# The last stage's norms: scalings of the sums moved from VectorE to GpSimd

## The chip, the cores and the metric

The kernel runs on one core of one Trainium2 chip. The metric is the device time of one execution in microseconds; the median of several runs is compared. Five engines take part, each with a queue of its own and tied to the others by semaphores: TensorE (PE in the rows, its weight loads PEld), VectorE (DVE), ScalarE (ACT), GpSimd (POOL), and SyncE (SP), which only starts DMAs.

## What is computed

A decoder layer for 16 sequences of 100 tokens of width 512: causal self attention, cross attention to a context of 361 tokens, and a feed-forward part with eight experts of which each token takes two; a layer norm follows each of the three. The change lies in the last part. Cut to it:

```python
combined = sum over the token's two experts of weight * silu(x @ expert_w[e] + expert_b[e])
out = combined @ proj_w + proj_b
y = x + out
rms = sqrt(mean(y * y) + 1e-6)                  # RMS norm
x = x + norm_w * (y / rms)
m, v = mean(x), var(x)
x = (x - m) / sqrt(v + 1e-5)                    # layer norm
```

All of it is float32. The matrix products are split in a high and a low part, three products for each.

## The kernel before

The kernel runs in three phases on the same core: self attention, cross attention, feed forward. The feed-forward phase sorts the 1600 tokens by expert into 32 slots of 128 rows, multiplies each by its expert's weights, and writes the results to DRAM (`y_d`). Then comes the last stage, which is all that the change touches.

The last stage goes over 13 tiles of tokens (`NT`), 12 of 128 rows and one of 64. A tile t takes this way:

- GpSimd gathers the two expert results of each row from `y_d` by indirect DMA (`gather_results`, L1903, two instructions a tile);
- ScalarE weighs the first (`weigh_first`, L1637), VectorE adds the weighed second (`combine`, L1803, a scalar_tensor_tensor);
- TensorE transposes the tile (L1577), ScalarE copies the high part (`combined_hi`, L1643), VectorE makes the low part (`combined_lo`, L1809);
- TensorE multiplies by the projection (12 matmuls at L71 and a bias matmul at L1599);
- VectorE adds the residual (`residual`, L1817), ScalarE squares and sums (`square`, L1649) into `ss`;
- VectorE adds the constant to the sum (`mean_square`, L1822), GpSimd raises it to -0.5 (`rms`, L1909) into `rr`;
- VectorE multiplies by it and by the norm's weights (`rms_norm`, L1828, a scalar_tensor_tensor), adds the input and sums (L1831), and makes the negative mean (L1834);
- ScalarE sums the squared deviations (`deviation`, L1654) into `dev`;
- VectorE makes the variance (`variance`, L1839), GpSimd raises it to -0.5 (`ln`, L1914) into `rstd`;
- VectorE makes the shift (`mean_shift`, L1844), ScalarE applies the layer norm (`layer_norm`, L1660), and SyncE stores the tile.

The mean squares, variances, roots and shifts work on one column, a number per row. The order of the work is written out by hand: each engine has one loop over t, in which the steps of different tiles stand behind one another, and it takes them strictly in this order. VectorE's iteration t is: `combine(t + 1)`, `combined_lo(t)`, `mean_square(t - 2)`, `residual(t - 1)`, `mean_shift(t - 4)`, `variance(t - 3)`, `rms_norm(t - 2)`. ScalarE's is: `weigh_first(t + 1)`, `combined_hi(t)`, `deviation(t - 3)`, `square(t - 1)`, `layer_norm(t - 4)`. GpSimd gathers tiles 0 to 4 first; its iteration t is `gather_results(t + 5)` (two indirect DMAs, as long as there are tiles), `rms(t - 1)`, `ln(t - 2)`. So the last gather, of tile 12, stands in front of the root of tile 6. TensorE transposes one tile ahead.

The semaphore `ms_set` counts the mean squares and is what `rms` waits for; `var_set` does the same for `ln`. `sq_done` and `dev_done` count ScalarE's sums.

Of the kernel before, what the change touches and what calls it, by code (L numbers as in the profile page):

```python
# [22 lines left out]
ALU = mybir.AluOpType  # L23
# [4 lines left out]
B, S, D = 16, 100, 512  # L28
DC = D // P
BIG = 3.0e38  # L30
LN_EPS = 1e-5
RMS_EPS = 1e-6
# [13 lines left out]
NT = 13  # L46
# [10 lines left out]
def wait(eng, sem, value):  # L57

    if not isinstance(value, int) or value > 0:
        eng.wait_ge(sem, value)  # L60
# [1323 lines left out]
def feed_forward_phase(nc, sem, bank, stage, rank_set, x2_out, x2_d, y_d, pick_d, expert_w, Ehl, expert_b, proj_w, proj_b, norm_w,  # L1384
# [8 lines left out]
    with ExitStack() as ctx:  # L1393
# [18 lines left out]
        ss, rr, rstd = [[small[:, 4 + k * NT + t:5 + k * NT + t] for t in range(NT)] for k in range(3)]  # L1412
        usum, neg_mean, dev, shift = [[small[:, 4 + k * NT + t:5 + k * NT + t] for t in range(NT)] for k in range(3, 7)]
# [52 lines left out]
        ms_set, var_set, shift_set = sem("c_ms_set"), sem("c_var_set"), sem("c_shift_set")  # L1466
        u_rdy, sq_done, rr_set, norm_step, dev_done = sem("c_u_rdy"), sem("c_sq_done"), sem("c_rr_set"), sem("c_norm_step"), sem("c_dev_done")
# [6 lines left out]
        def rows(t):  # L1474
            return P if t < NT - 1 else B * S - P * (NT - 1)
# [202 lines left out]
        def _(dve):  # L1678
# [121 lines left out]
            def combine(t):  # L1800
                n = rows(t)
                dve.wait_ge(r_w1, t + 1)
                dve.scalar_tensor_tensor(out=r_s[0:n, 0, t], in0=r_s[0:n, 1, t], scalar=weight_of(t, 1), in1=r_s[0:n, 0, t],  # L1803
                                         op0=ALU.mult, op1=ALU.add).then_inc(c_rdy, 1)

            def combined_lo(t):
                n = rows(t)
                dve.wait_ge(c_hi, t + 1)
                dve.tensor_tensor(cTl[:, t % 2, :, 0:n], t_bank[t % 2][:].rearrange("p (c t) -> p c t", c=DC)[:, :, 0:n],  # L1809
                                  cTh[:, t % 2, :, 0:n].bitcast(F32), ALU.subtract).then_inc(c_lo, 1)  # L1810

            def residual(t):
                n = rows(t)
                dve.wait_ge(p_done, t + 1)
                if t % 3 == 0:
                    dve.wait_ge(x2_in[t // 3], 16)
                dve.tensor_tensor(u_s[0:n, t], p_bank[t % 2][0:n, :], x2_tile(t), ALU.add).then_inc(u_rdy, 1)  # L1817

            def mean_square(t):
                n = rows(t)  # L1820
                dve.wait_ge(sq_done, t + 1)
                dve.tensor_scalar(rr[t][0:n, :], ss[t][0:n, :], D * RMS_EPS, None, ALU.add).then_inc(ms_set, 1)  # L1822

            def rms_norm(t):
                n = rows(t)
                u = u_s[0:n, t]
                dve.wait_ge(rr_set, t + 1)
                dve.scalar_tensor_tensor(out=u, in0=u, scalar=rr[t][0:n, :], in1=nw_s[0:n, :], op0=ALU.mult,  # L1828
                                         op1=ALU.mult).then_inc(norm_step, 1)
                dve.wait_ge(norm_step, 2 * t + 1)  # L1830
                dve.tensor_tensor_reduce(out=u, in0=u, in1=x2_tile(t), scale=1.0, scalar=0.0, op0=ALU.add, op1=ALU.add,  # L1831
                                         accum_out=usum[t][0:n, :]).then_inc(norm_step, 1)
                dve.wait_ge(norm_step, 2 * t + 2)
                dve.tensor_scalar(neg_mean[t][0:n, :], usum[t][0:n, :], -1.0 / D, None, ALU.mult).then_inc(mv_set, 1)  # L1834

            def variance(t):
                n = rows(t)
                dve.wait_ge(dev_done, t + 1)
                dve.tensor_scalar(rstd[t][0:n, :], dev[t][0:n, :], 1.0 / D, LN_EPS, ALU.mult, ALU.add).then_inc(var_set, 1)  # L1839

            def mean_shift(t):
                n = rows(t)
                dve.wait_ge(rstd_set, t + 1)
                dve.tensor_tensor(shift[t][0:n, :], neg_mean[t][0:n, :], rstd[t][0:n, :], ALU.mult).then_inc(shift_set, 1)  # L1844
# [7 lines left out]
            for t in range(NT + 4):  # L1852
                if t < 2:
                    combined_lo(t)
                if t + 1 < NT:
                    combine(t + 1)
                if 2 <= t < NT:
                    combined_lo(t)
                if 2 <= t <= NT + 1:
                    mean_square(t - 2)  # L1860
                if 1 <= t <= NT:
                    residual(t - 1)
                if t >= 4:
                    mean_shift(t - 4)
                if 3 <= t <= NT + 2:
                    variance(t - 3)
                if 2 <= t <= NT + 1:
                    rms_norm(t - 2)

        @block.gpsimd  # L1870
        def _(pool):
            def split_lo(n):
                pool.wait_ge(w_hi, n + 1 - 2 * PRE)
                pool.tensor_tensor(pieces[n][3], pieces[n][1], pieces[n][2].bitcast(F32), ALU.subtract).then_inc(w_lo[0], 1)

            def gather_slots(j):
                wait(pool, gt_done, j - 2 * NG + 1)
                pool.indirect_dma_start(out=xg[:, j % (2 * NG)], out_offset=None, in_=x2_f,
                                        in_offset=bass.IndirectOffsetOnAxis(ap=tok_s[:, j:j + 1], axis=0)).then_inc(xg_in[j % (2 * NG)], 16)

            pool.memset(ones_s, 1.0).then_inc(set_up, 1)
            pool.memset(half_s, -0.5).then_inc(set_up, 1)
            for k in range(2):
                pool.memset(run[k][:], 0.0).then_inc(set_up, 1)
                pool.memset(tend[k][:], 0.0).then_inc(set_up, 1)
            pool.wait_ge(x2_out, 16 * B)
            pool.wait_ge(tok_set, 1)
            for j in range(NJ):
                gather_slots(j)
                if j == 2 * NG - 1:  # L1890
                    split_lo(2 * PRE)
                    split_lo(2 * PRE + 2)
                if j == 2 * NG:
                    split_lo(2 * PRE + 4)
                if j in (2 * NG + 2, 2 * NG + 3):
                    split_lo(2 * (LATE + j - 2 * NG - 2))
                if j in (2 * E, 2 * E + 1):
                    split_lo(j)

            def gather_results(t):  # L1900
                n = rows(t)
                for k in range(2):
                    pool.indirect_dma_start(out=r_s[0:n, k, t], out_offset=None, in_=y_d,  # L1903
                                            in_offset=bass.IndirectOffsetOnAxis(ap=pick_s[0:n, t, k:k + 1], axis=0)).then_inc(r_in[t], 16)

            def rms(t):
                n = rows(t)
                pool.wait_ge(ms_set, t + 1)
                pool.tensor_tensor(rr[t][0:n, :], rr[t][0:n, :], half_s[0:n, :], ALU.pow).then_inc(rr_set, 1)  # L1909

            def ln(t):
                n = rows(t)
                pool.wait_ge(var_set, t + 1)
                pool.tensor_tensor(rstd[t][0:n, :], rstd[t][0:n, :], half_s[0:n, :], ALU.pow).then_inc(rstd_set, 1)  # L1914

            pool.wait_ge(h_done, NJ)
            pool.wait_ge(set_up, 2)
            pool.wait_ge(pick_in, 32)
            for slot in y_out:
                pool.wait_ge(slot, 16 * NJ // 2)  # L1920
            for t in range(5):
                gather_results(t)
            for t in range(NT + 2):
                if t + 5 < NT:
                    gather_results(t + 5)
                if 1 <= t <= NT:
                    rms(t - 1)
                if 2 <= t:
                    ln(t - 2)
# [105 lines left out]
```

## Time and profile before

| | us |
|---|---|
| median of 3 runs | 1572.05 (1570.88 to 1576.07) |
| the profiled execution | 1567.09 |
| its span in the trace | 1565.3 |
| TensorE busy | 1478.7 (94%) |
| VectorE busy | 949.5 (61%) |
| ScalarE busy | 662.7 (42%) |
| GpSimd busy | 648.6 (41%) |

The busy times are sums over the whole span, over stages with different limits. The last stage begins with the first gather at 1492.64 us and takes up what is left of the span. Times in the rows below count from the span's start.

### The profile page before, as it was taken

The numbers are of one execution on the slowest core, as the hardware profiler recorded it, in microseconds if no ns is written. First come the engines' busy times: TensorE is split into PE (matmuls) and PEld (weight loads), VectorE is DVE, ScalarE is ACT, GpSimd is POOL, SyncE is SP. The second block draws the span as 40 slices with busy tenths as digits, with TensorE's granted clock in tenths as the row PEclk, the third lists the DMA queues.
The fourth block names the chain that finished last, engine by engine and source line by source line (L and its number), as shares of the span: only waits on it lengthen the run. The fifth ranks groups of instructions, "written<-read, shape, count | busy, mean of one in ns | idle before, by whom it ended". The sixth has DMA issues, their size and how long they took to land. (4 is left out here: it accounts for less than half of the span.)

```text
span 1565.3 us, 28124 instructions
## 1 busy us (share of the span) xinstructions
PE 1478.7 (94%) x8673; PEld 1214.4 (78%) x8673; DVE 949.5 (61%) x3585; ACT 662.7 (42%) x1789; POOL 648.6 (41%) x1000
## 2 busy tenths in 40 slices
PE   8999999999999889999999999999999999479996
PEld 7777877877876678888888888888888887367874
DVE  3766566666666676556655666557655665654457
ACT  4443334334343354444434444434444445343346
POOL 1334334324434454434443444344444443374174
PEclk9999999999999999999999999999999999789998
DMA  6321221122142431212112111211121213365373
GB/s 212 110 72 63 90 78 63 73 85 72 52 141 92 151 115 38 72 51 62 52 53 62 56 55 43 61 56 55 43 62 56 65 40 117 135 212 185 124 233 117
DMA packets 60748, 139.76 MB, mean 89 GB/s; under 512 B 10165, under 2 KB 20761, under 8 KB 59666
## 3 DMA queue, kind: packets, MB, share of 16 engines
q1 hardware_dynamic: 56086, 123.85, 24.0%
q0 software_dynamic: 4576, 14.95, 3.3%
q8 instruction: 32, 0.52, 0.1%
q14 instruction: 54, 0.44, 0.1%
HBM read 94.31 MB, written 44.46 MB: 89 GB/s over the span
## 5 line engine op out<-in xcount | busy, mean ns | idle before, releaser
L1277 POOL TENSOR_TENSOR b_pcarry<-b_half 128x1 f32<-128x1 f32 x173 | 47.9, 277 | 387.5 <-DVE b_rinv L1147 349.8
L1035 ACT ACTIVATE b_probs<-b_probs,b_nmax 100x361 f32<-100x361 f32 x256 | 152.1, 594 | 81.5 <-DVE b_nmax L1141 81.1
L71 PE MATMUL bank<-b_kTh,b_q 128*100 128x362 f32 x512 | 171.8, 337 | 9.1 <-DVE b_kTl L1123 5.8
L1141 DVE CUSTOM_DVE_ANT_0 b_probs<-bank,b_mask 100x361 f32<-100x361 f32 x256 | 135.5, 529 | 52.8 <-issue 45.0
L1302 POOL TENSOR_SCALAR b_probs<-b_probs,b_rinv 100x361 f32<-100x361 f32 x256 | 163.3, 651 | 0.0
L1134 DVE TENSOR_TENSOR b_pTl<-bank,b_pTh 121x400 fp32r<-121x400 f32 x192 | 109.7, 572 | 50.9 <-ACT b_pTh L1030 50.9
L1030 ACT ACTIVATE b_pTh<-bank 121x400 fp32r<-121x400 f32 x192 | 96.5, 503 | 88.4 <-PE bank L867 84.2
L1076 ACT ACTIVATE b_oTh<-bank,b_bv 128x400 fp32r<-128x400 f32 x64 | 38.1, 595 | 223.1 <-PE bank L71 223.1
L867 PE MATMUL bank<-ident,b_probs 100*121 100x100 f32 x768 | 109.8, 265 | 4.3 <-POOL b_probs L1302 3.3
L867 PEld LDWEIGHTS bank<-ident,b_probs 100*121 100x121 f32 x768 | 106.6, 185 | 7.1 <-POOL b_probs L1302 4.5
L71 PE MATMUL bank<-b_Woh,b_oTh 128*100 128x512 f32 x256 | 110.7, 432 | 1.4 <-DVE b_oTl L1205 1.4
L71 PEld LDWEIGHTS bank<-b_kTh,b_q 128*100 128x100 f32 x512 | 85.0, 166 | 29.5 <-issue 13.8
L71 PE MATMUL bank<-a_Wqh,a_x1Th 128*100 128x512 f32 x256 | 100.7, 394 | 2.7 <-DVE a_qn L560 1.5
L71 PE MATMUL bank<-a_Wqh,a_x1Tl 128*100 128x512 f32 x256 | 101.0, 394 | 0.0
L71 PE MATMUL bank<-b_Woh,b_oTl 128*100 128x512 f32 x256 | 100.7, 393 | 0.0
L71 PE MATMUL bank<-a_Wql,a_x1Th 128*100 128x512 f32 x256 | 100.6, 393 | 0.0
L71 PE MATMUL bank<-b_Wol,b_oTh 128*100 128x512 f32 x256 | 100.6, 393 | 0.0
L1205 DVE SCALAR_TENSOR_TENSOR b_oTl<-bank,b_bv,b_oTh 128x400 fp32r<-128x400 f32 x64 | 40.6, 634 | 96.9 <-ACT b_oTh L1076 96.9
L437 ACT ACTIVATE a_probs<-a_probs,a_nmax 100x100 f32<-100x100 f32 x256 | 92.8, 367 | 4.4 <-DVE a_nmax L513 4.4
L640 POOL TENSOR_TENSOR a_probs<-a_probs,a_rinv 100x400 f32<-100x400 f32 x64 | 54.7, 855 | 93.0 <-DVE a_rinv L520 93.0
L71 PE MATMUL bank<-b_Wkh,b_ctxh 128*121 128x512 f32 x192 | 80.4, 419 | 7.0 <-DVE b_kn L1104 6.5
L71 PE MATMUL bank<-b_kTl,b_q 128*100 128x362 f32 x256 | 84.2, 329 | 0.0
(259 smaller groups left out, 3963.1 us busy)
## 6 DMA issues: line engine op xcount, KB each, us to landing
b_q<-q_d SPq DMA_DIRECT2D x64, 400.0 KB, 3.2
q_d<-a_qo SPq DMA_DIRECT2D x62, 400.0 KB, 2.4
b_ctxr<-in_ctxT SPq DMA_DIRECT2D x48, 242.0 KB, 4.0
y_d<-c_y SPq DMA_DIRECT2D x32, 256.0 KB, 3.5
c_Eraw<-in_expert_w SPq DMA_DIRECT2D x10, 512.0 KB, 7.7
a_stage<-in_Wq SPq DMA_DIRECT2D x4, 1024.0 KB, 5.2
stage<-in_Wo SPq DMA_DIRECT2D x8, 512.0 KB, 4.5
a_xTr<-in_xT SPq DMA_DIRECT2D x8, 400.0 KB, 3.1
```

The source lines that it names most:

```text
L71: mm = eng.matmul(out, lhsT=l(c), rhs=r(c), start=first and k == 0, stop=last and k == n - 1)
L437: e = act.activation(probs[:, r, c, :], probs[:, r, c, :], ACT.Exp, scale=-1.0, bias=nmax[:, h:h + 1], accum_out=psums[:, r, c:c + 1])
L640: pool.tensor_tensor(probs[:, r], probs[:, r], rinv[:, r].unsqueeze(2).to_broadcast([S, DC, S]), ALU.mult).then_inc(pn_rdy, 1)
L867: mm = pe.transpose(t_bank[c % 2][0:KT, h * S:(h + 1) * S], probs[:, s % 2, h, c * KT:(c + 1) * KT], ident_s[0:S, 0:S])
L1030: act.activation(pTh[:, c, :], t_bank[c % 2][0:KT, 0:XG * S], ACT.Copy).then_inc(pt_hi, 1)
L1035: act.activation(p, p, ACT.Exp, scale=-1.0, bias=nmax[:, s % 2, h:h + 1], accum_out=psums[:, s % 2, h:h + 1]).then_inc(e_rdy, 1)
L1076: act.activation(oTh[:, kv, :], o_bank[:, 0:XG * S], ACT.Identity, bias=bv_s[:, kv:kv + 1]).then_inc(o_hi, 1)
L1134: dve.tensor_tensor(pTl[:, c, :], t_bank[c % 2][0:KT, 0:XG * S], pTh[:, c, :].bitcast(F32), ALU.subtract).then_inc(pt_lo, 1)
L1141: dve.tensor_tensor_reduce(out=probs[:, s % 2, h, 0:SE], in0=s_bank[h % 2][0:S, 0:SE], in1=mask_s[:], scale=-1.0, scalar=BIG, op0=ALU.add, ...
L1205: dve.scalar_tensor_tensor(out=oTl[:, kv, :], in0=o_bank[:, 0:XG * S], scalar=bv_s[:, kv:kv + 1], in1=oTh[:, kv, :].bitcast(F32), op0=ALU.add,
L1277: pool.tensor_tensor(pcarry[:, k:k + 1], half_s[:, 0:1], half_s[:, 0:1], ALU.add)
L1302: pool.tensor_scalar(p, p, rinv[:, s % 2, h:h + 1], 1.0, ALU.mult, ALU.mult).then_inc(p_rdy, 1)
```

## The change

The scalings of both sums move from VectorE's queue to GpSimd's. `mean_square` and `variance` leave VectorE's loop. Their instructions, the same operations on the same tiles with the same constants, stand in `rms` and `ln` now, each directly in front of the root. They wait for ScalarE's sum (`sq_done`, `dev_done`), and the root waits for `ms_set` or `var_set` as before, which GpSimd itself now raises. Everything else stays.

```diff
-            def mean_square(t):
-                n = rows(t)
-                dve.wait_ge(sq_done, t + 1)
-                dve.tensor_scalar(rr[t][0:n, :], ss[t][0:n, :], D * RMS_EPS, None, ALU.add).then_inc(ms_set, 1)
-            def variance(t):
-                n = rows(t)
-                dve.wait_ge(dev_done, t + 1)
-                dve.tensor_scalar(rstd[t][0:n, :], dev[t][0:n, :], 1.0 / D, LN_EPS, ALU.mult, ALU.add).then_inc(var_set, 1)
...
-                if 2 <= t <= NT + 1:
-                    mean_square(t - 2)
                 if 1 <= t <= NT:
                     residual(t - 1)
                 if t >= 4:
                     mean_shift(t - 4)
-                if 3 <= t <= NT + 2:
-                    variance(t - 3)
                 if 2 <= t <= NT + 1:
                     rms_norm(t - 2)
...
             def rms(t):
                 n = rows(t)
+                pool.wait_ge(sq_done, t + 1)
+                pool.tensor_scalar(rr[t][0:n, :], ss[t][0:n, :], D * RMS_EPS, None, ALU.add).then_inc(ms_set, 1)
                 pool.wait_ge(ms_set, t + 1)
                 pool.tensor_tensor(rr[t][0:n, :], rr[t][0:n, :], half_s[0:n, :], ALU.pow).then_inc(rr_set, 1)
 
             def ln(t):
                 n = rows(t)
+                pool.wait_ge(dev_done, t + 1)
+                pool.tensor_scalar(rstd[t][0:n, :], dev[t][0:n, :], 1.0 / D, LN_EPS, ALU.mult, ALU.add).then_inc(var_set, 1)
                 pool.wait_ge(var_set, t + 1)
                 pool.tensor_tensor(rstd[t][0:n, :], rstd[t][0:n, :], half_s[0:n, :], ALU.pow).then_inc(rstd_set, 1)
```

## Rows read from the trace of the kernel before

**Rows 1.** Busy time by stretches: us of each engine, TensorE's granted clock, DMA

```profile
core 0: us, PE busy (x) PEld busy (x) DVE busy (x) ACT busy (x) POOL busy (x), PEclk, DMA share, GB/s
1520.00:1535.00 15.00, 14.81 (x64) 9.86 (x63) 13.61 (x38) 11.45 (x25) 12.51 (x15) 1.00 0.78 253
```

**Rows 2.** Chain that ended last, one tile: start us, us, what

```profile
1526.13 0.61 DVE c_u L1817
...
1527.49 0.71 ACT c_u L1660
1528.20 0.62 ACT c_r L1637
1528.85 0.52 DVE c_r L1803
...
1530.26 0.61 DVE c_u L1817
```

**Rows 3.** GpSimd's timeline: start us, us, operation, idle time before it

```profile
1510.48 0.58 POOL L1909 TENSOR_TENSOR c_small<-c_small 128x1 f32<-128x1 f32 x1
...
1523.54 1.00 POOL L1903 DMA_INDIRECT c_r<-y_d,c_pick  x1 [0.17 <-issue]
1524.84 1.47 POOL L1903 DMA_INDIRECT c_r<-y_d,c_pick  x1 [0.30 <-issue]
1526.33 0.57 POOL L1909 TENSOR_TENSOR c_small<-c_small 128x1 f32<-128x1 f32 x1
1526.94 0.55 POOL L1914 TENSOR_TENSOR c_small<-c_small 128x1 f32<-128x1 f32 x1
...
1534.52 0.56 POOL L1909 TENSOR_TENSOR c_small<-c_small 128x1 f32<-128x1 f32 x1 [0.56 <-DVE c_small L1822]
```

**Rows 4.** VectorE's timeline in the same period

```profile
1524.72 0.75 DVE L1803 SCALAR_TENSOR_TENSOR c_r<-c_r,c_pick 128x512 f32<-128x512 f32 x1 [0.24 <-ACT c_r L1637]
...
1525.99 0.14 DVE L1822 TENSOR_SCALAR c_small<-c_small 128x1 f32<-128x1 f32 x1
1526.05 0.68 DVE L1817 TENSOR_TENSOR c_u<-bank,c_x2b 128x512 f32<-128x512 f32 x1
...
1526.94 0.75 DVE L1828 SCALAR_TENSOR_TENSOR c_u<-c_u,c_small,stage 128x512 f32<-128x512 f32 x1
...
1528.46 0.15 DVE L1834 TENSOR_SCALAR c_small<-c_small 128x1 f32<-128x1 f32 x1
```

**Rows 5.** The timeline of both engines after the last gather

```profile
1539.36 1.02 POOL L1914 TENSOR_TENSOR c_small<-c_small 128x1 f32<-128x1 f32 x1 [0.18 <-DVE c_small L1839]
...
1539.22 0.75 DVE L1828 SCALAR_TENSOR_TENSOR c_u<-c_u,c_small,stage 128x512 f32<-128x512 f32 x1
```

**Rows 6.** GpSimd's prices in earlier phases: timeline, and groups (busy us, mean ns)

```profile
108.86 0.19 POOL L659 TENSOR_TENSOR a_rstd<-a_mv,a_ln_eps 100x1 f32<-100x1 f32 x1 [11.32 <-DVE a_mv L609]
109.13 0.56 POOL L661 TENSOR_TENSOR a_rstd<-a_rstd,a_half 100x1 f32<-100x1 f32 x1
...
L1283 POOL TENSOR_SCALAR b_ctxh<-b_ctxr 128x484 fp32r<-128x484 f32 x45 | 26.9, 597 | 0.0
```

**Rows 7.** The timelines of VectorE, ScalarE and GpSimd at the end

```profile
1555.98 0.14 DVE L1844 TENSOR_TENSOR c_small<-c_small 128x1 f32<-128x1 f32 x1
1556.88 0.15 DVE L1839 TENSOR_SCALAR c_small<-c_small 128x1 f32<-128x1 f32 x1 [0.76 <-ACT c_junk L1654]
1556.95 0.73 DVE L1828 SCALAR_TENSOR_TENSOR c_u<-c_u,c_small,stage 64x512 f32<-64x512 f32 x1
...
1554.86 0.19 ACT L1649 ACTIVATION_READ_ACCUMULATOR c_junk<-c_u 64x1 f32 x1
...
1559.25 0.18 ACT L1654 ACTIVATION_READ_ACCUMULATOR c_junk<-c_u,c_small 64x1 f32 x1
...
1559.69 0.54 POOL L1914 TENSOR_TENSOR c_small<-c_small 64x1 f32<-64x1 f32 x1 [1.60 <-DVE c_small L1839]
```

**Rows 8.** The timeline where gathers follow on gathers

```profile
1500.95 0.75 DVE L1803 SCALAR_TENSOR_TENSOR c_r<-c_r,c_pick 128x512 f32<-128x512 f32 x1
...
1501.40 1.12 POOL L1903 DMA_INDIRECT c_r<-y_d,c_pick  x1 [0.30 <-issue]
```

## The prediction

> **What bounds the kernel now.** The change touches the last stage alone, so I first looked in the timelines for where that stage lies: about 1499 to 1563 us of a span of 1565.3. Nothing before it can move. Inside the stage the view of busy time by stretches [rows 1] has TensorE at its full granted clock and VectorE busy for 13.6 of 15 us, so VectorE looks like the bound. The chain of waits says it more exactly [rows 2]: from one residual addition of VectorE (L1817) to the next are 4.13 us. Between them lie ScalarE's square (in the chain only as a gap), its layer norm (L1660) and its weighing (L1637), then VectorE's combination (L1803), its low split (L1809) and the next addition. That is a ring over two engines. An instruction of VectorE in this ring delays every tile; one behind the addition has cover, because the combination waits for ScalarE anyhow (0.24 us before L1803) [rows 4].
>
> GpSimd is not in that chain, and a look at its timeline is what decides this case. While it still issues gathers it has no gap worth the name [rows 3]: gather 1.00, gather 1.47, root 0.57, root 0.55, and between them 0.30 and 0.17 of issue, 4.12 in all. This is the same period as the ring's. So for the tiles 0 to 6 two engines are at their limit together, and a change that moves work from the one to the other must be costed on both. From tile 7 on the gathers are gone and GpSimd idles.
>
> One number in it is soft. The second gather takes 1.47, a free one 0.95 [rows 8]. Where a scalar_tensor_tensor of VectorE began shortly before a gather or a root, the GpSimd operation ends about 0.61 us after that instruction's start plus its own free time: the combination started at 1524.72, plus 0.61 and 0.95 gives 1526.28; read 1526.31 [rows 3, 4]. The root at 1539.36 beside a multiplication started at 1539.22: 1539.83 plus 0.55 gives 1540.38; read 1540.38 [rows 5]. A root that starts in the same hundredths as the multiplication is not held (1526.94, 0.55) [rows 3, 4]. I take this as a rule of the trace: held until 0.61 after the start. So GpSimd has about 0.5 us of slack in a period, hidden in a gather that would be held anyway.
>
> **VectorE's part.** Out go 13 mean squares (L1822) and 13 variances (L1839). They are pipelined: the one at 1525.99 lasts 0.14, but the addition behind it starts 0.06 later [rows 4]. The mean square stands in front of the addition, in the ring: 0.06 a tile. The variance stands behind it, and its 0.07 only widens the wait for ScalarE: nothing. The ring becomes 4.06.
>
> **GpSimd's part.** In come 26 small tensor_scalar, each in front of its root and with a wait for the root on it. The trace has no tensor_scalar so small on GpSimd. The nearest row is an addition in front of a root of the same shape in the first stage: 0.19 long, the root 0.27 behind its start (0.19 and a gap of 0.08) [rows 6]. From above it is bounded by the tensor_scalar over 484 columns, 0.60 [rows 6], from below by nothing, if it vanished in the held gather. I take 0.27, the same work but for the immediates, and keep both ends for the range. The new waits (square done, deviation done) are long met while the gathers last: the square fills the gap between the addition's end at 1526.74 and the layer norm at 1527.49 [rows 2], and its root is reached one period later. So no gather is queued behind a wait for ScalarE.
>
> Call R the end of the root of the RMS norm; VectorE's multiplication starts 0.04 behind it (1526.90 and 1526.94), its combination 1.59 behind the multiplication when ScalarE is early (the small product at 1528.46 is over at 1528.61, 1.67 behind, and instructions overlap by 0.08) [rows 3, 4]. With the change GpSimd's iteration is:
> - scaling for the layer norm starts at R + 0.04 together with the multiplication, so it is not held, 0.19; the root would start at R + 0.31 but is held to R + 0.65, and ends at R + 1.20;
> - first gather R + 1.37, 1.00; 0.30; second gather R + 2.67. The combination started at R + 1.63 and holds until R + 2.24: over. So the gather takes 0.95, to R + 3.62;
> - scaling and root of the next tile, 0.02 + 0.27 + 0.56: R + 4.47.
>
> The period is 4.47 while there are gathers, 0.35 more than now, and GpSimd is the bound in place of the ring: of the 0.54 added and 0.34 of a newly held root, 0.5 is eaten by the slack. The first tile's root ends 0.27 later. Between the first and the second lie the gathers without a layer norm: both gathers held as before, the scaling 0.27 more, so about 4.03. Now R goes from 1511.06 (tile 0) to 1535.08 (tile 6) [rows 3], 24.0 in six steps; after it is 1511.3 + 4.03 + 5 x 4.47 = 1537.7, that is 2.6 later. VectorE then gives back what it waits at that place now: the combination of tile 10 is free 1.59 behind the multiplication and not 2.02 behind it: 2.6 - 0.4 = 2.2. Two periods of 4.06 for 4.12 to tile 12: 2.2 - 0.1 = 2.1 later at TensorE's last products, which follow on each other.
>
> **The end.** There the order in VectorE's queue costs something now: the variance of tile 11 waits 0.76 for ScalarE, and the multiplication of tile 12 stands behind it, at 1556.95 [rows 7]. Its sum of squares was there at 1555.05 (1554.86 + 0.19). With the change the root of tile 12 needs nothing of VectorE: 1555.10, scaling 0.27, root 0.55, over at 1555.92, and the multiplication follows the small product of 1555.98 or takes its place: 1555.99. That is 0.96 earlier. Behind it the last deviation's scaling costs GpSimd what it saves VectorE: now from 1559.43 to the root's end at 1560.23 are 0.80, then 0.04 + 0.27 + 0.55 = 0.86 [rows 7]. So the end gains 0.9.
>
> **The sum** is 2.1 - 0.9 = 1.2 us. The profiled execution took 1567.09 (span 1565.3 and 1.8 around it): 1568.3. It lies 4.96 under the median of 1572.05; on the median: **1573.2**.
>
> Here a rule of the Trainium skill may be weighed. "GPSIMD Engine Reference", section "Key points", has GpSimd contend for its SBUF interfaces with VectorE instructions in a 2-port perf mode or with two SBUF inputs. The held operations above agree for the scalar_tensor_tensor, whose two inputs lie in SBUF. By this rule the reduction L1831 (two SBUF inputs too) would hold GpSimd as well; no row of mine starts a GpSimd operation inside it. In the steady iteration none does after either. At the end the scaling of tile 12 would start with it, at 1555.10, and be held for 0.5: 1.7 us in all in place of 1.2, which is no other outcome.
>
> **The rivals.**
> 1. *GpSimd has real slack, faster by 1.4 us.* The second gather's 1.47 might be 0.95 of work and 0.5 of waiting for the mean square: the root starts 0.34 after each L1822. Then the 0.54 nearly fit, the period is 4.06, and of nine periods 0.5 is gained, with the end 1.4: 1570.6. Against it: a gather with another gather behind it, which waits for nothing, takes 1.12 when a combination began at 1500.95: 1501.56 + 0.95 = 1502.51, read 1502.52 [rows 8]. Chance 0.17.
> 2. *The scaling is dear, slower.* If each costs 0.6 as the wide one does [rows 6], the RMS part of the iteration is 0.41 longer and the layer norm's root starts at R + 0.71, after the hold: the period is 4.94. Six steps give 1511.7 + 4.4 + 5 x 4.94 = 1540.8, 5.7 later; less 0.4 and 0.1 is 5.2; the end gains 0.1 only. That is 5.1, 1577.2. It decides from about 0.56 for one scaling, and holding both scalings behind multiplications does the same. Against it: the small addition of the first stage took 0.19 [rows 6], and a hold needs a start behind the multiplication's. Chance 0.10. With roots and gathers held besides, 8 us are the end of it: 1580.
> 3. *Nothing is gained at the end,* since the store of the last tile or another order takes its place: 2.1, 1574.2, inside the forecast's own range. Chance 0.10.
>
> The forecast has 0.63. TensorE's clock I don't count: it is granted 1.00 in the loop [rows 1], and no row there shows it lower.
>
> **How the numbers follow.** The forecast's own range is 1572 to 1575. The range has to take in rival 1 below and most of rival 2 above, and the three runs of before themselves spread from 1.2 under to 4.0 over their median: 1569.5 to 1577.5. A measurement of this kernel tells about 0.3% (4.7 us) from no change. The forecast and the rivals 1 and 3 lie within it, rival 2 at its edge: faster 0.02, within 0.90, slower 0.08.
>
> **What would show it.** Right: on GpSimd a period of about 4.4 to 4.5 for tiles 1 to 6, small scalings of 0.2, roots of the layer norm held (about 0.9), second gathers at 0.95 and not 1.47; on VectorE an idle stretch of about 0.9 in front of L1828 put down to GpSimd's root; from tile 7 on 4.06; the last multiplication about 1.65 behind the one before it (which ran at 1554.34) and not 2.6. Wrong: a period of 4.06 from the start (rival 1), scalings of 0.6 (rival 2), or a wait of GpSimd for ScalarE in front of a gather.

## The result and the profile after

| | before | after |
|---|---|---|
| median, us | 1570.41 (9 runs, 1565.89 to 1576.07) | 1577.61 (9 runs, 1575.37 to 1581.32) |
| ratio of the times | | 1.0046, 95% interval 1.0032 to 1.0060 |
| profiled execution, us | 1567.09 | 1578.09 |
| its span, us | 1565.3 | 1575.9 |

The change costs 7.2 us by the medians, or 0.46%, and the interval of the ratio lies clear of 1. I had forecast 1.2, and the measured 1577.6 lies 0.1 above the upper end of my range. (The forecast of 1573.2 was added up on the first three runs of before, with their median of 1572.05. On the median of nine it would be 1571.6.) The spans differ by more, 10.6, but 2.8 of that are older than the change: the first gather starts at 1495.40 and not at 1492.64. So the comparison below is of a part that both traces share: from the start of the first multiplication of the RMS norm (L1828 before, L1823 after) to the end of the last layer norm. It takes 50.2 us before (1511.10 to 1561.27) and 57.9 after (1514.00 to 1571.92). I call it **the run of the tiles**.

GpSimd's timeline over one period, after (start us, us, operation), beside [rows 3]:

```profile
1529.18 0.75 POOL L1902 TENSOR_SCALAR c_small<-c_small 128x1 f32<-128x1 f32 x1
1530.02 1.00 POOL L1904 TENSOR_TENSOR c_small<-c_small 128x1 f32<-128x1 f32 x1
1531.20 1.21 POOL L1889 DMA_INDIRECT c_r<-y_d,c_pick  x1 [0.18 <-issue]
1532.71 0.95 POOL L1889 DMA_INDIRECT c_r<-y_d,c_pick  x1 [0.30 <-issue]
1533.69 0.25 POOL L1895 TENSOR_SCALAR c_small<-c_small 128x1 f32<-128x1 f32 x1
1534.02 0.57 POOL L1897 TENSOR_TENSOR c_small<-c_small 128x1 f32<-128x1 f32 x1
1534.67 0.75 POOL L1902 TENSOR_SCALAR c_small<-c_small 128x1 f32<-128x1 f32 x1
```

and VectorE's in the same period, beside [rows 4]:

```profile
1529.13 0.75 DVE L1823 SCALAR_TENSOR_TENSOR c_u<-c_u,c_small,stage 128x512 f32<-128x512 f32 x1 [1.90 <-POOL c_small L1897]
1529.92 0.69 DVE L1826 CUSTOM_DVE_ANT_0 c_u<-c_u,c_x2b 128x512 f32<-128x512 f32 x1
1530.54 0.08 DVE L1826 DVE_READ_ACCUMULATOR2_ANT c_small<- 128x1 f32 x1
1530.65 0.15 DVE L1829 TENSOR_SCALAR c_small<-c_small 128x1 f32<-128x1 f32 x1
1530.73 0.74 DVE L1803 SCALAR_TENSOR_TENSOR c_r<-c_r,c_pick 128x512 f32<-128x512 f32 x1
...
1534.63 0.75 DVE L1823 SCALAR_TENSOR_TENSOR c_u<-c_u,c_small,stage 128x512 f32<-128x512 f32 x1 [1.90 <-POOL c_small L1897]
```

Three things are to be seen. The period is 5.50 (1529.13 to 1534.63), where 4.13 stood and I had forecast 4.47. VectorE waits 1.90 us of it for GpSimd's root. And GpSimd's operations fall one after the other into VectorE's: the scaling at 1529.18 starts 0.05 behind the multiplication and takes 0.75; the root at 1530.02 starts 0.10 behind the reduction L1826 and takes 1.00 in place of 0.55; the gather at 1531.20 starts inside the combination and takes 1.21 in place of 0.95. From there on GpSimd is free of VectorE, since VectorE waits for it.

TensorE has a second surprise, also in the changed kernel, in the view of busy time by stretches (us of each engine, then TensorE's granted clock), beside [rows 1]:

```profile
1532.00:1535.00 3.00, 3.00 (x14) 2.17 (x12) 1.10 (x4) 2.30 (x5) 2.50 (x5) 1.00 0.51 118
1535.00:1538.00 3.00, 1.59 (x8) 0.95 (x8) 2.93 (x7) 1.04 (x3) 2.63 (x3) 1.00 0.39 153
1538.00:1541.00 3.00, 3.00 (x10) 2.33 (x9) 1.07 (x4) 2.52 (x5) 2.52 (x5) 0.58 0.62 169
...
1550.00:1553.00 3.00, 3.00 (x10) 2.13 (x8) 2.02 (x5) 2.33 (x5) 1.66 (x4) 0.64 0.23 87
```

and in its chain of waits:

```profile
1548.57 4.56 PE bank L71 x12
1553.13 0.45 PE bank L1599
1553.60 0.70 DVE c_u L1817
```

The clock falls from its upper level of 2.4 GHz to 1.2 (0.58 and 0.64 are means over stretches that have both) behind periods of 5.50 in which TensorE worked for 4.1 and was idle for 1.4 (the expectations below have 1.6). A product of twelve matmuls then takes 4.56 and not 3.1, most of it at the lower level. The one at 1538 was hidden in a period of 5.5; the one at 1548.57 was the first behind the last gather, and the addition waited for it. The multiplications there stand at 1549.05 and 1554.27, 5.22 apart in place of 4.1.

### The profile page after: what moved, and what is told of

It is laid out like the page before. It is cut to its first block and busy times, and to the rows that moved or that the text cites. A ratio compares the mean times of both kernels' runs of the same rounds, so it can differ in the third digit from the quotient of the medians.

```text
span 1575.9 us, 28124 instructions
## 1 busy us (share of the span) xinstructions
PE 1483.9 (94%) x8673; PEld 1218.7 (77%) x8673; DVE 947.6 (60%) x3559; ACT 663.3 (42%) x1789; POOL 658.8 (42%) x1026
## 5 line engine op out<-in xcount | busy, mean ns | idle before, releaser
L1134 DVE TENSOR_TENSOR b_pTl<-bank,b_pTh 121x400 fp32r<-121x400 f32 x192 | 109.7, 572 | 50.9 <-ACT b_pTh L1030 50.9
```

Source lines behind the costliest of these rows:

```text
L1134: dve.tensor_tensor(pTl[:, c, :], t_bank[c % 2][0:KT, 0:XG * S], pTh[:, c, :].bitcast(F32), ALU.subtract).then_inc(pt_lo, 1)
```

## The experiments

All twelve ran later, in three groups of four. There the kernel before takes 1579.5 to 1581.2 us, some 10 more. The trace of the kernel before from one of these groups (below) shows where most of it lies: at the stage's start ScalarE, VectorE and TensorE stand still for 6 to 7 us each, 4.7 of them all three together, and the first multiplication comes 26.1 us behind the first gather and not 18.5. This gap turned out to matter for the change, so I give for each run the run of the tiles beside the ratio. The traces of all twelve have the gap (first multiplication 26.0 to 34.4 us behind the first gather). Each run of the tiles comes from one trace.

| kernel | run of the tiles, us | longest periods | ratio (95%) |
|---|---|---|---|
| before, first runs | 50.2 | 4.13 | 1 |
| whole change, first runs | 57.9 | 5.51 | 1.0046 (1.0032 to 1.0060) |
| before again | 50.3 | 4.25 | 1.0001 (0.9986 to 1.0016) |
| mean square alone | 50.6 | 4.66 | 0.9998 (0.9983 to 1.0013) |
| variance alone | 54.2 | 5.30 | 1.0026 (1.0009 to 1.0042) |
| no scaling | 49.1 | 4.07 | 0.9992 (0.9980 to 1.0004) |
| late tiles only | 50.0 | 4.24 | 1.0002 (0.9986 to 1.0017) |
| whole change again | 51.7 | 5.50, one | 1.0019 (1.0000 to 1.0038) |
| with 8 matmuls | 60.7 | 5.65 | 1.0070 (1.0044 to 1.0097) |
| layer norm first | 59.8 | 5.00 | 1.0076 (1.0052 to 1.0101) |
| scaling as an addition | 50.9 | 4.67 | 1.0006 (0.9995 to 1.0017) |
| no lead | 56.8 | 5.51 | 1.0047 (1.0030 to 1.0064) |
| no lead, 3 matmuls | 56.9 | 5.51 | 1.0042 (1.0023 to 1.0062) |
| seven tiles ahead | 49.8 | 4.63, one | 1.0047 (1.0029 to 1.0066) |

**The parts alone.** The theory of the hold: the loss is made by GpSimd's operations falling into VectorE's with two SBUF inputs. Its rival, of the price: each scaling costs the same wherever it stands.

Mean square alone (VectorE keeps the variance):

```diff
-                if 2 <= t <= NT + 1:
-                    mean_square(t - 2)
...
+                pool.wait_ge(sq_done, t + 1)
+                pool.tensor_scalar(rr[t][0:n, :], ss[t][0:n, :], D * RMS_EPS, None, ALU.add).then_inc(ms_set, 1)
                 pool.wait_ge(ms_set, t + 1)
```

> Only the mean square moves to GpSimd, the variance stays on VectorE. Compared is the stage, from the start of the first gather to the end of the last layer norm: 68.6 us before, 76.5 with the whole change. Theory of the hold (GpSimd's operations are held by VectorE's instructions with two SBUF inputs, and it is the layer norm's scaling and root that fall into them): the root of the layer norm still starts with the multiplication and isn't held, so the period with gathers is the old one plus little, 4.1 to 4.2, and the stage is 69 to 70 us; time within 1 us of before. Theory of the price (each scaling costs its length and a gap, wherever it stands): half of the added 1.4 us a period, 4.8, and a stage of 72.5.

Variance alone (VectorE keeps the mean square):

```diff
-                if 3 <= t <= NT + 2:
-                    variance(t - 3)
...
+                pool.wait_ge(dev_done, t + 1)
+                pool.tensor_scalar(rstd[t][0:n, :], dev[t][0:n, :], 1.0 / D, LN_EPS, ALU.mult, ALU.add).then_inc(var_set, 1)
                 pool.wait_ge(var_set, t + 1)
```

> Only the variance moves to GpSimd, the mean square stays on VectorE. Theory of the hold: scaling held to about 0.75, root held to about 1.0, first gather held: period with gathers 5.1 to 5.2, stage 74.5 to 75.5 us, time about 6 us over before: nearly all of the loss. Theory of the price: 4.8, 72.5 us, the same as for the mean square alone.

The gap puts the stage's length out of use (77.8 and 82.7 us from the first gather), so the expected lengths can't be read off; the periods can. With the mean square alone they are 4.09 to 4.12 after one of 4.66. With the variance alone they are 5.30, 5.13, 5.13 and 5.04, as the theory of the hold has it, though only four of them, and so 3.9 us in all and not 6; the theory of the price wanted 4.8 for both. Against the kernel before with the gap (50.3) the run of the tiles grows by 0.3 and by 3.9. So the variance on GpSimd is what costs, and the mean square is nearly free by itself. GpSimd's timeline of the first of them shows why:

```profile
1546.67 0.25 POOL L1907 TENSOR_SCALAR c_small<-c_small 128x1 f32<-128x1 f32 x1
1547.01 0.57 POOL L1909 TENSOR_TENSOR c_small<-c_small 128x1 f32<-128x1 f32 x1
1547.56 0.54 POOL L1914 TENSOR_TENSOR c_small<-c_small 128x1 f32<-128x1 f32 x1
```

The layer norm's root follows on the other root by 0.00 and so still starts 0.05 ahead of VectorE's multiplication (at 1547.61). It isn't held.

No scaling at all (the roots are taken of the raw sums):

```diff
-                pool.wait_ge(ms_set, t + 1)
-                pool.tensor_tensor(rr[t][0:n, :], rr[t][0:n, :], half_s[0:n, :], ALU.pow).then_inc(rr_set, 1)
+                pool.wait_ge(sq_done, t + 1)
+                pool.tensor_tensor(rr[t][0:n, :], ss[t][0:n, :], half_s[0:n, :], ALU.pow).then_inc(rr_set, 1)
```

and the same for the variance.

> Neither engine scales: the roots are taken of the raw sums, straight behind ScalarE's (this leaves the constants and the division by 512 out of both norms). What is left is the change without GpSimd's 26 instructions. If the whole loss comes from what GpSimd gets, this is faster than before: period 4.06, the end 0.9 shorter, a stage of 67.0 to 67.5 us. If the earlier start of the roots itself moves them into VectorE's instructions, the period with gathers stays over 4.2 and the stage over 68.6.

From the third period to the ninth they are 4.06 or 4.07, and the end (last residual addition to last layer norm) takes 6.7 and not 7.7. That is what taking the scalings off VectorE is worth when nobody has them: 0.06 a tile in the ring, as predicted, and 0.95 at the end. The predicted 0.9 at the end was for a GpSimd that does scale, and that it doesn't show. The run of the tiles is 1.2 shorter than before with the gap. So the loss comes wholly from what GpSimd gets.

Late tiles only:

```diff
-                if 2 <= t <= NT + 1:
+                if 2 <= t <= 8:
                     mean_square(t - 2)
...
-                if 3 <= t <= NT + 2:
+                if 3 <= t <= 8:
                     variance(t - 3)
...
+                if t >= 7:
+                    pool.wait_ge(sq_done, t + 1)
...
+                if t >= 6:
+                    pool.wait_ge(dev_done, t + 1)
```

> Both scalings move to GpSimd only where it has no gathers left: mean square from tile 7 on, variance from tile 6 on. Tiles before are scaled by VectorE. GpSimd has room there (idle over 2 us a period), so nothing is lost; gained are 0.06 a tile in the ring for some four tiles and up to 0.9 at the end. Theory of the hold: stage 67.5 to 68.3 us, time 0.3 to 1.1 us below before, too little for the comparison of times, to be read in the trace. If the loss lay in the scalings' price alone or in the end, the stage would be over 68.6.

Nothing is lost where GpSimd has no gathers: 50.0 against 50.3 us. The gain of 0.3 is at the lower edge of what was expected, since the end takes 7.3 us and not 6.7 (see the end below). The ratio can't tell it from nothing.

**The same kernel, another loss.** The changed kernel, unchanged, once more:

> The changed kernel once more, as the yardstick for the next three on the same chip. Read is the part from the first multiplication of the RMS norm to the end of the last layer norm: 50.2 us before, 57.9 with the change. Theories of the hold and of the clock both expect the same as before: period with gathers 5.5, about 58 us, one product of TensorE of about 4.5 us in place of 3.0 behind the last loaded periods. If this long product was an accident of one execution, 56.8.

Neither came true. The whole change has here a run of the tiles of 51.7 us; its periods are 3.82, 3.87, 4.08, 4.64, 5.50, 4.59 and then 3.5 to 4.1. The full 5.50 is there just once. By the ratio the time is about 3 us over the kernel before's (0 to 6) where the first runs had 7; the two intervals overlap, so it is the traces that tell the two apart. That made the theory of the lead: in the gap at the stage's start GpSimd does its gathers, arrives early at the first scaling and waits there for ScalarE:

```profile
1518.50 0.25 POOL L1895 TENSOR_SCALAR c_small<-c_small 128x1 f32<-128x1 f32 x1 [5.88 <-ACT c_junk L1649]
```

That is 2.5 us ahead of the first multiplication (1521.00). With no gap the first scaling starts 1.0 ahead (1513.02 and 1514.00) and has nothing to wait for. So with the gap GpSimd is ahead of VectorE, which it may be since its scaling needs ScalarE's sum alone; without it GpSimd arrives just in time, and every period is paid for from the first.

No lead, and the kernel before, unchanged, as yardstick:

```diff
                 pool.wait_ge(sq_done, t + 1)
+                if t == 0:
+                    pool.wait_ge(c_lo, 3)
```

> The kernel before once more, as the yardstick on this chip. From the first multiplication of the RMS norm to the end of the last layer norm 50.2 us, periods 4.1. If this chip too has VectorE, ScalarE and TensorE stand still together for some 8 us at the start of the stage, the same gap is in this kernel, and it isn't of the change. The theory of the lead (below) gives the kernel before no use of the gap: its roots wait for VectorE's mean squares, so it stays at 50.2.

> The whole change, but GpSimd waits in front of the first scaling until the low part of tile 2 is made, which is the place where VectorE made the mean square before. Theory of the lead: with the 8 us gap GpSimd is a period ahead of VectorE when the tiles begin to run, and that lead is used up at 1.4 us a period before anything is late (periods 3.8, 3.9, 4.1, 4.6 and then 5.5 in the whole change there). Without the lead: one period of 4.1 to 4.6, then five of 5.4 to 5.5, and from the first multiplication to the end 57 to 58 us in place of 51.7, time 6 to 8 us over before. If the milder loss on this chip has another cause: 51.7 again.

Both came true in the main. The kernel before has the gap as well:

```profile
ACT c_cTh L1643 <- remote: 13.4, 2, 7.4
...
DVE c_cTl L1809 <- issue: 7.2, 1, 7.2
PEld bank L71 <- issue: 6.3, 1, 6.3
PE bank L71 <- issue: 6.1, 1, 6.1
```

(its waits at the start of the stage: who waited for whom, us in total, times, longest). The run of the tiles is 50.3 in spite of it. One wait added in front of one instruction gives the periods 4.14, 5.51, 5.50, 5.50, 5.49, 5.41, which in the first trace of the change are 4.13, 5.51, 5.49, 5.50, 5.49, 5.41, and 56.8 us, 0.2 under the expected 57 to 58. The ratio is 1.0047, as in the first runs (1.0046). So the lead is shown to be what made the loss mild.

How it does so is not as I expected. The lead is no full period: in the whole change again the RMS root of the first tile ends 1.6 us ahead of its multiplication, those of the next three 1.0, 0.5 and 0.2 ahead, and those of the three behind them 0.04. So it is used up at 0.2 to 0.6 us a period and not at 1.4. Yet the run of the tiles is 5 us shorter than without it (51.7 against 56.8). While there is a lead, GpSimd's own period is not 5.5 but, from root to root, 4.41, 4.34, 4.40 and 4.82, near the forecast's 4.47: GpSimd is ahead of the multiplication, and the layer norm's scaling is not held (0.19 in the first three). The third of them, and VectorE's multiplication beside it:

```profile
1532.65 0.19 POOL L1902 TENSOR_SCALAR c_small<-c_small 128x1 f32<-128x1 f32 x1
...
1532.77 0.73 DVE L1823 SCALAR_TENSOR_TENSOR c_u<-c_u,c_small,stage 128x512 f32<-128x512 f32 x1
```

So the lead avoids the hold more than it pays for it. The 4.59 in this trace, 0.9 of the 5 us, comes from something else. Its scaling starts 0.05 behind the multiplication, as all the held ones do, and is not held all the same:

```profile
1542.91 0.78 DVE L1823 SCALAR_TENSOR_TENSOR c_u<-c_u,c_small,stage 128x512 f32<-128x512 f32 x1 [1.90 <-POOL c_small L1897]
1542.96 0.19 POOL L1902 TENSOR_SCALAR c_small<-c_small 128x1 f32<-128x1 f32 x1
```

Of thirty scalings that start 0.05 behind a multiplication, over all traces, this is the one that is let through. So at that distance the start decides nearly always, but not by itself.

**The clock.** Matmuls of a small size in a free bank, in the time that TensorE idles:

```diff
+                if 3 <= t <= 9:
+                    keep_busy(pe, bank[4][:, 0:P], ident_s, 8)
                 pe.wait_ge(c_lo, t + 1)
```

> The whole change, and TensorE runs 8 small matmuls (0.9 us) in a free bank in front of its wait for the low part, for the tiles 3 to 9 only, where a period of 5.5 leaves it idle for 1.6. Theory of the clock (TensorE is granted the low clock after the loaded periods, since it idles more, and one product is late by it): granted clock 1.00 throughout, no product over 3.1 us, the long period of 5.2 becomes 4.1, in all 1.1 to 1.3 us less, 56.7. If the clock has no part in it: 58, or more by the matmuls that come in the way.

This run says nothing of the clock's cost, for I had sized it wrong. Each of these float32 matmuls is two in the trace:

```profile
1541.28 1.95 PE L79 MATMUL bank<-ident 128*128 128x128 f32 x16
```

1.95 us and not 0.9: TensorE became the bound, with seven periods of 5.59 to 5.65 (and a granted clock of 1.00 in them). Smaller, and on the kernel without a lead:

```diff
+                if 4 <= t <= 9:
+                    keep_busy(pe, bank[4][:, 0:P], ident_s, 3)
                 pe.wait_ge(c_lo, t + 1)
```

> As the kernel without a lead, and TensorE runs 3 small float32 matmuls (about 0.7 us) in a free bank in front of its wait for the low part, for the tiles 4 to 9. They fit in the 1.6 us that it idles in a loaded period. Theory of the clock: granted clock 1.00 all through the stage, no product of 4.5 us, and 0.5 to 1.2 us less than without the filler if a slow product falls behind the loaded periods there. If the fall of the clock doesn't depend on the idle time: the same products of 4.5 us, or the time is longer by the matmuls.

Busy time by stretches, without the matmuls and with them, at the same place (the second stretch of the first pair is busy throughout because its product is a slow one):

```profile
1540.00:1545.00 5.00, 3.60 (x14) 2.42 (x13) 3.31 (x8) 2.83 (x7) 4.32 (x6) 0.87 0.65 210
1545.00:1550.00 5.00, 5.00 (x19) 3.46 (x18) 3.53 (x8) 2.85 (x7) 4.32 (x6) 0.79 0.46 138
```

```profile
1540.00:1545.00 5.00, 4.05 (x22) 3.23 (x22) 3.07 (x8) 3.13 (x7) 4.31 (x6) 1.00 0.54 170
1545.00:1550.00 5.00, 4.06 (x22) 3.04 (x21) 3.14 (x8) 2.85 (x7) 4.32 (x6) 1.00 0.44 146
```

So the fall of the clock comes from the idle time: without the extra matmuls TensorE works for 4.1 us of each period of 5.50 and the clock falls to 1.2 GHz twice, with them it works for 4.6 and the clock stays at 1.00 throughout, in one trace of each. Its price is not constant. In this pair it is nothing (56.8 and 56.9), because both slow products fell inside loaded periods. In the first profiled execution one fell behind them: 57.9 against 56.8 with otherwise equal periods, so about 1.1 us, in that one trace.

**Order and hold.** The layer norm's pair in front of the RMS norm's, on GpSimd:

```diff
-                if 1 <= t <= NT:
-                    rms(t - 1)
                 if 2 <= t:
                     ln(t - 2)
+                if 1 <= t <= NT:
+                    rms(t - 1)
```

> The whole change, but GpSimd takes the layer norm's scaling and root (tile t-2) in front of the RMS norm's (tile t-1). The number of instructions is the same. Theory of the hold: the layer norm's pair then runs while VectorE waits for GpSimd, unheld (0.25 and 0.57 in place of 0.75 and 1.00), while the first gather falls into the multiplication (about 1.5) and the second into the combination: a period of 5.0 to 5.1 in place of 5.5, six of them: 55 to 56 us, and less clock loss. Theory of the price: nothing changes, 5.5 and 58 us.

```profile
1534.36 1.57 POOL L1889 DMA_INDIRECT c_r<-y_d,c_pick  x1 [0.16 <-issue]
1536.24 1.16 POOL L1889 DMA_INDIRECT c_r<-y_d,c_pick  x1 [0.30 <-issue]
1537.47 0.19 POOL L1902 TENSOR_SCALAR c_small<-c_small 128x1 f32<-128x1 f32 x1
1537.74 0.56 POOL L1904 TENSOR_TENSOR c_small<-c_small 128x1 f32<-128x1 f32 x1
1538.30 0.24 POOL L1895 TENSOR_SCALAR c_small<-c_small 128x1 f32<-128x1 f32 x1
...
1564.74 0.19 POOL L1902 TENSOR_SCALAR c_small<-c_small 128x1 f32<-128x1 f32 x1 [2.65 <-ACT c_junk L1654]
```

On the hold it is as expected: the pair takes 0.19 and 0.56 where it took 0.75 and 1.00, the gather behind the multiplication takes 1.57, and the period is 4.99. The time is a miss all the same, 59.8 us. The first period is 4.5 and the loaded ones behind it are 5.0, so the early start of GpSimd helps little here; I put that down to the order, as the RMS norm's root now waits for the layer norm's, but no run shows it. And behind the last gather a new ring is the bound: GpSimd waits 2.65 us for the deviation with the next root queued behind it, and all later periods are 4.3, to the very end. I hadn't asked what is queued behind that wait.

The scaling as an addition:

```diff
-                pool.tensor_scalar(rstd[t][0:n, :], dev[t][0:n, :], 1.0 / D, LN_EPS, ALU.mult, ALU.add).then_inc(var_set, 1)
+                pool.tensor_tensor(rstd[t][0:n, :], dev[t][0:n, :], half_s[0:n, :], ALU.add).then_inc(var_set, 1)
```

> The whole change, but the layer norm's scaling is a tensor_tensor addition of a constant column (this leaves the division by 512 and the constant out and adds -0.5 to the sum). A tensor_tensor followed on a root by 0.00 to 0.04 us, a tensor_scalar by 0.08, which is behind the start of VectorE's multiplication (0.04 behind the root). If who starts first decides the hold: the scaling is unheld, 0.2, its root starts inside the multiplication and ends 1.20 behind the RMS root in place of 1.92, period 4.6 to 4.8, 53.5 to 54.5 us. If the hold doesn't depend on that start: scaling 0.75 as before, 5.5, 58 us.

```profile
1545.20 0.57 POOL L1897 TENSOR_TENSOR c_small<-c_small 128x1 f32<-128x1 f32 x1
1545.75 0.18 POOL L1902 TENSOR_TENSOR c_small<-c_small 128x1 f32<-128x1 f32 x1
1546.01 0.96 POOL L1904 TENSOR_TENSOR c_small<-c_small 128x1 f32<-128x1 f32 x1
1547.14 1.04 POOL L1889 DMA_INDIRECT c_r<-y_d,c_pick  x1 [0.18 <-issue]
...
1545.80 0.75 DVE L1823 SCALAR_TENSOR_TENSOR c_u<-c_u,c_small,stage 128x512 f32<-128x512 f32 x1 [1.06 <-POOL c_small L1897]
```

An operation that starts at 1545.75, 0.05 ahead of the multiplication, is not held; one at 1529.18, 0.05 behind it, was. The loaded periods are 4.67, inside the expected 4.6 to 4.8. So 0.8 us a period hang on a gap of 0.08 in place of 0.00 between two GpSimd instructions of different forms. It is the start that counts and not the form: the scaling at 1532.65 above is a tensor_scalar, starts 0.12 ahead and is not held either. The run of the tiles is 50.9 where the whole change has 51.7; the expected 53.5 to 54.5 were for a run without the lead.

Seven tiles ahead:

```diff
-            for t in range(5):
+            for t in range(7):
                 gather_results(t)
...
-                if t + 5 < NT:
-                    gather_results(t + 5)
+                if t + 7 < NT:
+                    gather_results(t + 7)
```

> The whole change, with 7 tiles gathered in front of the loop in place of 5, so that two fewer iterations carry gathers. Theory of the lead: in executions with the gap the two tiles are gathered inside it, the lead of some 4 us lasts nearly to the last gather, and at most one period is over 4.2: 49.5 to 50.5 us from the first multiplication to the end, 1.5 to 2 less than the whole change. In an execution without the gap the first multiplication comes about 5 us later instead. If the loss is of the roots and scalings and not of the gathers beside them: 51.7.

On the run of the tiles it is right: 49.8 us, one period of 4.63, all others under 4.1. But the first multiplication comes 34.4 us behind the first gather and not 26: the start of the stage grew by 8 us for four more gathers, which I had thought would hide in the gap. ScalarE, VectorE and TensorE stand still together a second time there, for 5.0 us from 1518.57 on. For the first 1.6 of them GpSimd still issues its gathers in front of the first scaling. By the medians it is 7.7 us slower than before. None of the kernels that compute all of both norms is measurably faster than the kernel before.

## Why the prediction was wrong

**What held.** The ring's 4.06 is what no scaling at all shows. GpSimd did become the bound while it has gathers, with the wait of VectorE for its root, and no gather was queued behind a wait for ScalarE. The price of a scaling that is not held was nearly right: 0.25 to 0.29 long for the RMS norm's and 0.19 for the layer norm's, and 0.08 of gap to the root (I took 0.27 with the gap, so 0.06 too little for the RMS norm's). A slip without effect: the six terms that I gave for GpSimd's period before add up to 4.06 and not to 4.12; the rest are gaps of a few hundredths.

**The step that failed** is the first of the list of GpSimd's iteration, "scaling for the layer norm starts at R + 0.04 together with the multiplication, so it is not held". It starts at R + 0.08, behind the multiplication's R + 0.03, and is held. The 0.04 that I used was the gap of a root behind a root; I had no row of a tensor_scalar behind a root. Counted from R, the root's end:

| | predicted | measured |
|---|---|---|
| layer norm's scaling ends | 0.23 | 0.83 |
| its root ends | 1.20 | 1.92 |
| first gather ends | 2.37 | 3.31 |
| second gather ends | 3.62 | 4.56 |
| next root's end, the period | 4.47 | 5.49 |

The root, which I had held by the multiplication to 1.20, starts inside the reduction instead and is held again. Here the Trainium skill's rule ("GPSIMD Engine Reference", section "Key points": contention with VectorE instructions that have two SBUF inputs) was right where I had only half used it: I had written that in the steady iteration nothing starts inside the reduction, and by my wrong start nothing did. The trace agrees with it now, 1.00 for a root of 0.55 in six periods. One hold of 0.56 made the next two: I had read from rows of 0.01 us what starts with what, and built a chain of three operations on it. The other order stood only in half a sentence of my second rival ("holding both scalings behind multiplications does the same"), with its upper end of 8 us if roots and gathers were held besides. That end is what came, but the rival's own sum (a period of 4.94, 5.1 us) and its chance of 0.10 rested on the scaling's price, which was not it.

**The sum again, from the traces.** Six steps from the first tile's root to the seventh's take 31.5 us and not 24.0; I had 26.4, so 5.1 are missing there. Where I had 0.4 given back behind the last gather it is 0.6 (3.52 in place of 4.10). The slow product costs 1.1. I had set the clock aside with the argument that the loop before shows none lower, which is no argument on a loop that idles more. The end gains 0.35 of the 0.9 (7.67 to 7.32 from the last residual addition). The root of the layer norm in front of the last pair takes 1.56:

```profile
1564.86 1.56 POOL c_small L1904
1566.42 0.40 POOL c_small L1895
```

That root alone is not what the end costs. With 8 matmuls and with the scaling as an addition it takes 0.99 and 1.00, and the end is 7.34 and 7.32 all the same, because the last tile's scaling then starts 0.06 behind VectorE's reduction (at 1581.31) and is held:

```profile
1580.10 0.99 POOL L1906 TENSOR_TENSOR c_small<-c_small 128x1 f32<-128x1 f32 x1
...
1581.37 0.71 POOL L1897 TENSOR_SCALAR c_small<-c_small 64x1 f32<-64x1 f32 x1 [0.27 <-ACT c_junk L1651]
```

(with 8 matmuls). That is the hold of 0.5 that the prediction had weighed for this place and left out of its 1.2. One way or the other the multiplication of the last tile comes 2.2 us behind the one before it and not 1.65.

The forecast's 1.2 holds 0.27 for the first tile's root, which lies ahead of the run of the tiles. Without it, 0.93 + 5.1 - 0.2 + 1.1 + 0.55 = 7.5, and the run of the tiles grew by 57.9 - 50.2 = 7.7, so 0.2 is not accounted for; the medians differ by 7.2.

**What stays open.** The root of 1.56 starts at 1564.86, 0.41 ahead of VectorE's multiplication (1565.27). Roots of earlier tiles that start as far ahead take 0.55 (1557.91 in the same trace, 0.42 ahead), so it should have been let through. The same 1.56 stands at this place in seven traces (the change, variance alone, late tiles only, whole change again, both without a lead, seven tiles ahead) and 0.99 or 1.00 in two, so it is no accident, but no run takes it apart. Nor is it known why one scaling in thirty was let through. I also don't know what the three engines wait for in the gap at the stage's start, nor why they stood still a second time with seven tiles ahead. It is not of the change, since the kernel before has it. The load on the DMA engines alone is not it either: they are busy 0.99 at 351 GB/s in the gap of the kernel before (1504.10 to 1508.70), and just the same in its first trace from 1500.90 to 1505.50, where TensorE works for 4.4 of the 4.6 us. Whether it comes with the chip was not tried.

## What to carry to other kernels

Ask of each engine that gets work, not only of the one that is relieved, whether it has room in that very stage: GpSimd was busy for 41% of the span and for all of a period where it mattered. When two engines run in lockstep and one holds the other, work out who starts first to the hundredth, cost both orders, and treat a chain of such starts as one coin and not as a sum. At a few hundredths even the order is no certainty: the same start was let through once in thirty. And see whether the engine is ahead of the other or just in time at the start: with a lead the run of the tiles grew by 1.4 us (50.3 to 51.7; it would be 2.3 but for the one scaling let through), without it by 6.5 (50.3 to 56.8).

## What the runs showed of the hardware

- A GpSimd operation that starts behind a two-input instruction of VectorE takes its own time on top of what is left of about 0.6 us from that instruction's start: scaling 0.75 for 0.19, root 1.00 for 0.55, gather 1.57 for 0.95. Scalings that start 0.05 behind are held in 29 cases of 30. Those that start 0.05 ahead are let through (0.18, 0.54), and so are roots up to 0.5 ahead, with the exception above. Gathers that start 0.06 to 0.09 behind a scalar_tensor_tensor are let through too (0.90 to 0.96 in nine cases, 1.08 in one); those that start 0.10 to 0.16 behind take 1.41 to 1.59.
- On GpSimd a tensor_scalar follows on a root by 0.08 us, a tensor_tensor by 0.00 to 0.04.
- TensorE's granted clock fell to 1.2 GHz behind periods of 5.50 us in which it worked for 4.1, twice in each of the two traces with six such periods and nothing added (the change, no lead). It stayed at 1.00 with 4.6 us of work in the same period, and in loops with periods of 4.99 (layer norm first) and 5.13 (variance alone). A product of twelve in which it fell took 4.6 us, the others 3.0 to 3.1.
- ScalarE, VectorE and TensorE stood still together at the stage's start, with 26 indirect gathers in the stage, for 3.6 to 9.6 us in all, in all twelve later traces and in neither of the first two.
